# Two layer normalisations scaled on GpSimd instead of VectorE, with re-placed steps, in a fused attention kernel

## The reference, cut to what matters

```
x: (8, 1024, 256) float32
x = x + 0.5 * ffn(layernorm(x))        # "plain" pass, 8 batches
x = x + linear_attn(layernorm(x))      # products without a softmax
x = x + 0.5 * ffn(layernorm(x))        # "plain" pass again, 8 batches

layernorm(x) = (x - mean) / sqrt(var + 1e-5)          # no gain, no bias
ffn(x): q, k, v = x @ Wq, x @ Wk, x @ Wv              # 16 heads of 16
        a = softmax over q of (q k^T / 16)            # 1024 x 1024 per head
        z = a v; z = l2norm(z @ Wo); z = l2norm(z @ Wff); gelu(z)
linear_attn(x): q, k, v of w_qkv; out = (q k^T) v; out @ w_o^T + b_o
```

## Time and profile before

| what | value |
|---|---|
| time, 3 runs | median 2916.42 us (2914.94 to 2917.38) |
| the profiled execution | 2915.55 us, its span 2913.5 us |
| mean granted TensorE clock | 0.987 |
| busy share of the span | PE 92%, DVE 94%, ACT 93%, POOL 26% |

### The profile page before, as it was taken

How to read it: one execution, slowest core, us unless ns; L and a number is a source line. 1 busy time by engine, 2 the same in 40 slices (tenths; PEclk the granted TensorE clock), 3 DMA queues, 4 the chain that set the end, 5 groups by cost and what they waited for, 6 DMA issues and landing times.

```text
span 2913.5 us, 87438 instructions
## 1 busy us (share of the span) xinstructions
PE 2675.2 (92%) x35680; PEld 1077.5 (37%) x35680; DVE 2740.9 (94%) x5574; ACT 2720.2 (93%) x5031; POOL 750.6 (26%) x1181
## 2 busy tenths in 40 slices
...
GB/s 123 52 65 40 55 100 52 68 45 59 103 41 59 65 59 99 37 56 76 59 85 43 54 85 74 89 49 74 61 58 85 74 88 46 64 71 57 74 88 16
DMA packets 151362, 192.89 MB, mean 66 GB/s; under 512 B 34001, under 2 KB 85713, under 8 KB 150962
## 3 DMA queue, kind: packets, MB, share of 16 engines
q1 hardware_dynamic: 150386, 186.13, 31.1%
...
q0 software_dynamic: 576, 1.18, 0.3%
...
## 4 chain that ended last, share of the span: by engine, by line
PE 39%; DVE 36%; ACT 15%; issue 7%; SPq 2%; DMA 0%; POOL 0%; DVEq 0%; ACTq 0%; POOLq 0%
DVE exp_ring L664 30%; PE ring L774 14%; PE ring L828 12%; ACT exp_ring L579 11%; PE o_acc L839 11%; SPq L428 2%; PE ring L879 2%; ACT w_xn L590 1%; DVE bn_stats L704 1%; DVE x_prep L714 1%; DVE bn_stats L718 1%; DVE x_post L686 1%; ACT L590 1%; DVE w_xn L681 1%; DVE exp_rsums L674 1%
## 5 line engine op out<-in xcount | busy, mean ns | idle before, releaser
L664 DVE TENSOR_SCALAR_CACHE_REDUCE exp_ring<-ring 128x1024 f32<-128x1024 f32 x2048 | 2411.9, 1214 | 81.8 <-PE ring L828 74.5
L579 ACT ACTIVATE exp_ring<-exp_ring,neg_max 128x1024 f32<-128x1024 f32 x2048 | 2334.0, 1143 | 109.9 <-DVE exp_ring L664 104.7
L828 PE MATMUL ring<-kq_stack 128*32 128x512 bf16 x16384 | 1186.8, 383 | 172.0 <-DVE exp_ring L664 143.4
L839 PE MATMUL o_acc<-exp_ring,v_scaled 128*32 128x512 f32 x8192 | 1079.0, 599 | 4.8 <-DVE o_T L671 1.9
L828 PEld LDWEIGHTS ring<-kq_stack 128*32 128x32 bf16 x16384 | 409.5, 96 | 1109.0 <-DVE exp_ring L664 538.9
L532 POOL TENSOR_TENSOR v_scaled<-v_now,exp_rsums 128x64 f32<-128x64 f32 x512 | 151.6, 296 | 1911.1 <-DVE exp_rsums L674 1897.8
L579 ACT ACTIVATION_READ_ACCUMULATOR exp_ring<-exp_ring,neg_max 128x1 f32 x2048 | 387.5, 189 | 0.0
L839 PEld LDWEIGHTS o_acc<-exp_ring,v_scaled 128*32 128x32 f32 x8192 | 254.8, 110 | 219.3 <-issue 16.5
L774 PE MATMUL ring<-ffn_wo_wowff,o_T 128*32 128x256 f32 x4096 | 244.4, 380 | 22.3 <-DVE exp_ring L664 11.4
L774 PE MATMUL ring<-xn_T,ffn_wqkv 128*32 128x512 f32 x2048 | 245.0, 598 | 10.8 <-DVE exp_ring L664 9.7
L774 PEld LDWEIGHTS ring<-ffn_wo_wowff,o_T 128*32 128x32 f32 x4096 | 134.2, 110 | 128.2 <-DVE exp_ring L664 29.6
...
## 6 DMA issues: line engine op xcount, KB each, us to landing
...
```

Source lines behind the costliest of these rows:

```text
L579: nc.scalar.activation(e, e, ACT.Exp, bias=negmax[:, i % NM:i % NM + 1], scale=-1.0, accum_out=sums[:, g % EG, c:c + 1]).then_inc(exp_done, 1)
L664: nc.vector.tensor_scalar(E[:, (g % EG) * HQ + c, :].rearrange("p (b n) -> p b n", b=NB), ps, -1.0, None, ALU.mult, ALU.min, accum_out=neg ...
L828: last = mm(ps[k:k + COLS, n, :], kq[:, 0, c, j * P + k:j * P + k + COLS], kq[:, 1, c, n * BANK:(n + 1) * BANK], start=True, stop=True)
L839: last = mm(O[32 * c:32 * c + 32, n, :], vsc[a][:, g % EG, c, :], E[:, (g % EG) * HQ + c, n * BANK:(n + 1) * BANK], start=(a == 0 and j == ...
```

## The change

The `xn` step of phases 1 to 15 (120 instructions) and all `xn2` steps (64) are issued by GpSimd and no longer by VectorE. The eight `xn` of phase 0 stay on VectorE. Since a phase is prepared during the one before, the 120 run in phases 0 to 14, eight in each: 8 in phase 0, 64 in the linear phases, 48 in the plain phases 9 to 14; phase 15 has none. GpSimd adds a negated mean and multiplies by `rstd`; it makes the negated mean itself by one small instruction behind each `rstd` (24 in all), and the semaphore of `rstd` now counts two a step. Nearly all places of the tables and several leads are other numbers. No other instruction is added or removed.

```diff
+        negm = sb("neg_mean", [P, NT])
+        negm2 = sb("neg_mean2", [P, NT])
...
# GpSimd's walk
                 if kind == "ln_rstd":
                     pool.wait_ge(var_ready, p + 1)
                     nc.gpsimd.tensor_tensor(rstd[:], rstd[:], half_neg[:], ALU.pow).then_inc(rstd_ready, 1)
+                    nc.gpsimd.tensor_tensor(negm[:], zero[:, 0:1].to_broadcast([P, NT]), mv[:, :, 0],
+                                            ALU.subtract).then_inc(rstd_ready, 1)
+                elif kind == "xn" and p >= 1:
+                    pool.wait_ge(rstd_ready, (p + 1) * 2)
+                    nc.gpsimd.tensor_scalar(xp[:, i, :], xp[:, i, :], negm[:, i:i + 1], rstd[:, i:i + 1],
+                                            ALU.add, ALU.mult).then_inc(xn_ready, 1)
...
+                elif kind == "xn2":
+                    pool.wait_ge(rstd2_ready, (p + 1) * 2)
+                    nc.gpsimd.tensor_scalar(wb[:, i, 0:D], xr[:, i, :], negm2[:, i:i + 1], rstd2[:, i:i + 1],
+                                            ALU.add, ALU.mult).then_inc(xn2_ready, 1)
...
# VectorE's walk
-                elif kind == "xn":
-                    dve.wait_ge(rstd_ready, p + 1)
+                elif kind == "xn" and p == 0:
+                    dve.wait_ge(rstd_ready, 2)
...
-                elif kind == "xn2":
-                    dve.wait_ge(rstd2_ready, p + 1)
-                    nc.vector.tensor_scalar(wb[:, i, 0:D], xr[:, i, :], mv2[:, i, 0:1], rstd2[:, i:i + 1],
-                                            ALU.subtract, ALU.mult).then_inc(xn2_ready, 1)
...
# LINEAR, two of its lines
-            "xn2": (45.6, 47, 47.2, 47.2, 48.2, 48.2, 49.7, 49.9),
+            "xn2": (43.1, 43.9, 44, 44.2, 45.6, 45.9, 49.6, 50.1),
...
# PLAIN, one of its lines
-            "xn": (33.2, 34.8, 36.6, 45.9, 48.2, 50.9, 51.8, 58.9),
+            "xn": (35.1, 35.9, 42.1, 45.5, 46.3, 46.8, 47, 47),
```

More of the change, by code:

```diff
@@ L67, in build_macaron @@
             "av_next": 2,
[L68 to L76, removed]
-            "xn": (33.2, 34.8, 36.6, 45.9, 48.2, 50.9, 51.8, 58.9),
-            "xt": (60.2, 65.1),
-            "qk": (77.2, 84.4, 93.2, 102.5, 18.2, 24.1, 33.9, 36.1),
@@ L80, in build_macaron @@
[L80 to L87, removed]
+            "z": 4.7,
+            "u": (8.7, 10.9, 12.4, 21.6, 29.9, 42.2, 55.8, 58.2),
+            "u_norm": (63.4,),
+            "w_norm": (66,),
+            "gelu": (67,),
+            "x1": (69.8, 70.4, 72, 72.3),
+            "ln_stats": (5.8, 7.9, 9, 9, 10.5, 10.5, 16.1, 16.2),
@@ new lines, in build_macaron @@
+            "ln_aggr": (25.6,),
+            "ln_rstd": (32.3,),
+            "xn": (35.1, 35.9, 42.1, 45.5, 46.3, 46.8, 47, 47),
+            "xt": (62.2, 66.6),
+            "qk": (76.9, 84.2, 90.1, 101.7, 17.9, 25.6, 33.3, 37.3),
+            "v": (117.8, 123.9, 127.4, 3.4),
+            "load_xp": (3.6,),
+            "stack1": (5.9,),
+            "load_xr": (7.8,),
+            "stack2": (40,),
+            "stack3": (81.5,),
+            "stack0": (107.7,),
+            "store": (113.4,),
@@ L113, in build_macaron @@
[L113 to L124, removed]
+            "w_norm": (32.1,),
+            "gelu": (32.3,),
@@ new lines, in build_macaron @@
+            "ln_stats": (3.9, 12.5, 13.1, 15.6, 16.1, 17.8, 22.2, 23.6),
+            "ln_aggr": (26.6,),
+            "ln_rstd": (29.8,),
+            "xn": (30.7, 32.2, 32.5, 33, 33.8, 33.9, 34.3, 34.6),
+            "xt": (45.4, 47.1),
+            "qk": (79.3, 81.9, 94.9, 98.2, 32.1, 35.9, 38.4, 41.8),
+            "v": (112.9, 124.8, 127.1, 4.3),
+            "load_xp": (0.1,),
+            "stack1": (58.4,),
+            "load_xr": (58.2,),
+            "stack2": (60.2,),
+            "stack3": (79.6,),
@@ L125, in build_macaron @@
+            "stack0": (91.6,),
+            "store": (103.4,),
         },
         "TAIL": {
[L127 to L133, removed]
+            "u": (7.9, 8.9, 14.5, 30.4, 31.7, 51.3, 53.3, 67.3),
+            "u_norm": (17.5, 71.5),
+            "w_norm": (37.3, 76.8),
```

70 lines of the change are left out of this document (36 added, 34 removed).

## The result

The changed kernel takes 2880.16 us, median of 4 runs (2878.12 to 2883.21), the kernel before 2916.88 in its runs beside it: the ratio is 0.9876, 95% interval 0.9859 to 0.9893. That is 36.7 us less; 26 were forecast. The profiled execution took 2880.11 us with a span of 2878.3.

What follows compares the result with a forecast made beforehand. VectorE was taken as the bound where xn and xn2 lie, with ScalarE next and TensorE bounding linear phases from tile 56; 2915.55 - 26.2 + 0.3 = 2889.7 us, stated as 2890, range 2856 to 2923.

Steps and rivals of the forecast that it cites:

- Linear phases: Eight linear phases: 1.6 us gained in tiles 32 to 39, 0.4 in 40 to 47; 2.0 a phase, 16.0 together.
- nothing: Linear phases before tile 32 and after tile 48: no gain.
- Plain phases: Phases 9 to 14, tiles 32 to 63: ScalarE allows 1.4 us; 1.2 taken a phase, 7.2 together.
- the shifts: Other moved places: single steps move by about a tile; counted as zero, uncertain by 1 us a phase either way.
- Phase 0 and the start: Phase 0 gains 3.0 us from eight instructions leaving VectorE; the negated mean adds 0.3 before the first scores.
- The new instruction: Normalisation on GpSimd: 0.41 us each, between 0.20 and 1.17; two pointer operands might cost more.
- D: Linear phases, tiles 32 to 47: GpSimd becomes the bound above 0.65 us an instruction; 2944 us at 1.17; chance 0.17.
- Contention: Linear phases, tiles 32 to 39: VectorE's x1 slows beside GpSimd from 0.69 to 1.24 us, 2.2 a phase at worst.
- Case C: Linear phases: v_scaled 5 us late costs 2 us a phase, cancelling the 16.0; 2906, up to 2920; chance 0.19.
- the sign that the prediction had named for C: av waiting for v_scaled over 2 us a phase while VectorE waits for TensorE.
- Case B: Whole kernel: VectorE's relief of 75.5 us passes through in full, 2841 us, or 2856 with four fifths; chance 0.12.
- the part said to be TensorE's: Linear phases from tile 56 on: TensorE busy 84.8 of 85.4 us, so work taken off VectorE gives nothing.

Runs made afterwards that it cites:

- e2: The changed kernel with the earlier kernel's tables, gaps and leads, except xn at lead 0 and xn2 at lead -1.5 on GpSimd: 2893.54 us, ratio 0.9923.
- e1: The kernel before with the changed kernel's tables, gaps and leads, every normalisation still on VectorE: 2957.25 us, ratio 1.0141.
- e5: e1 with one row moved, xn2 at places 47 to 50.1 instead of 43.1 to 50.1: 2921.77 us, ratio 1.0019.
- e3: The changed kernel with the 64 xn issued during the linear phases back on VectorE: 2899.24 us, ratio 0.9944.
- e6: The changed kernel with the third late qk step of the linear phases at place 39.6 instead of 38.4: 2878.66 us, ratio 0.9869.
- e7: The changed kernel with GpSimd subtracting the mean in xn and xn2 instead of adding the negated mean: 2952.68 us, ratio 1.0126.
- e10: The changed kernel with ScalarE's lead for the qk steps 0.0 instead of 1.0: 2918.97 us, ratio 1.0012.
- e4: The changed kernel with the linear phases' xn spread over places 31.7 to 43 instead of 30.7 to 34.6: 2937.79 us, ratio 1.0077.
- e8: The changed kernel with each of the 120 xn on GpSimd computed twice in place: 2927.08 us, ratio 1.0038.
- e9: The changed kernel with xn and xn2 in several add, multiply and subtract forms, constants or columns as operands, to price each: 2883.47 us.
- e11: e6 with ScalarE's lead for the qk steps 0.5 instead of 1.0: 2906.09 us, ratio 0.9968.
- e12: e6 with two of the linear phases' xn moved from 32.2 and 32.5 to 33.2, behind v_scaled: 2876.9 us, ratio 0.9867.

## Why the prediction was right, and where its steps were not

*The sum.* 26.2 us of gain were forecast, 36.7 came. The direction held, and so did the cause: the engine alone gives 22.6 (e2). How the gain is spread over the stretches did not hold.

*Linear phases, 16.0 forecast, 16.6 measured.* The total is right by luck, since the working is not. The term was 1.6 us in tiles 32 to 39. There the phases 1, 7 and 8 gained 0.9, 0.9 and 0.6, and phases 2 to 6 lost 0.5 to 1.0. ScalarE's 16.2 us were taken as the end of the stretch, but in the changed kernel 17.0 to 17.1 of its busy time fall into it, parts of ten exponentials where it was eight; that left 0.9, and phases 2 to 6, where the clock fell, took longer than before. What made it up lies mostly where the prediction said "nothing": tiles 8 to 31 (1.0 us a phase less), 40 to 55 (1.2 less, 0.4 of it foreseen) and the last eight (0.3 less), against 0.3 more in the first eight. Of the 1.0, 0.6 is there in e2 with the old places: the stretch of the earlier trace rows holds seven `xn`, and the eighth stood ahead of it. By e2 the engine accounts for 1.3 us a phase, the places for the rest, within the 1 us that was allowed for them.

*Plain phases, 7.2 forecast, 17.4 measured.* This is the term that was mis-sized. It was capped by ScalarE's idle time in the earlier trace rows (1.4 us), over tiles 32 to 63 alone. These tiles gave 2.4 us a phase, in e2 as in the changed kernel: they take 39.5 us instead of 41.9, with ScalarE busy for all 39.5 where it was 40.5 before. So its busy time in a window is no fixed demand. In all the engine gives 1.8 us a phase (e2), and 1.1 come from the places, by the difference of 168.9 and 167.8. These 1.1 are in tiles 8 to 31 (1.2 less), which e1 and e5 show too. The prediction put the shifts at "about a tile", but the last plain `xn` moved from place 58.9 to 47 and `stack2` from 66.7 to 40. Tiles 32 to 39 of phase 10 are busy on ScalarE and TensorE from end to end:

```profile
1890.50:1900.80 10.30, 10.30 (x136) 3.64 (x132) 9.57 (x20) 10.30 (x19) 8.20 (x12) 1.00 0.01 2
```

*Phase 0 and the start.* 3.0 less and 0.3 more; measured 2.2 less and 2.1 more. The start cannot be put down to the change: with the changed START table the first tile came at 49.7 to 50.6 us in e1, e3, e5, e6, e7 and e10 and at 47.8 to 48.5 in e4, e8, e9, e11 and e12, and with the old one at 50.2 in e2. One profile of each kernel cannot tell 2 us here.

*The new instruction.* 0.41 us forecast, 0.56 measured: the two column operands, which the text named as the risk, cost 0.15 (e9). It stayed below the 0.65 from which D decides. e7, at 1.22 us, and e8, with each `xn` paid twice, show D's mechanism: they cost the linear phases alone. Where between 0.56 and 1.22 the gain ends, no run shows.

*Contention.* VectorE's two-input `x1` was put at up to 1.24 us, 2.2 us a phase; it took 0.72 in the mean, 0.905 at most, against 0.684 before, 2.1 us in the whole kernel:

```profile
L700 DVE SCALAR_TENSOR_TENSOR x_post<-w_xn,x_post 128x512 f32<-128x512 f32 x64 | 44.7, 717 | 17.5 <-ACT w_xn L604 17.3
```

The contention is there, but mostly on the other side: the five `xn` on GpSimd took 4.09 us instead of 5 x 0.55, because the two that met an `x1` took 1.51 and 0.99; the first split's L420, beside an `x1` as well, took 1.03 instead of 0.62. Of the 120 `xn` of L513, 106 took 0.55 to 0.57 us, nearly all of them beside VectorE's scores. The price that the prediction feared turned up in e7: there two `x1` in each linear phase ran beside the split's L420 and L422, and took 1.12 and 1.64 us. In each of these pairs the instruction that began later grew: the `xn` of 998.55 behind an `x1` of 998.32, in e7 the `x1` of 1034.42 behind an L422 of 1034.04. The Trainium skill's rule (GPSIMD Engine Reference, "Specifications") is that both engines contend when VectorE's instruction has two SBUF inputs; the traces agree. The Trainium skill's advice to keep elementwise work on VectorE ("Engine selection") would have been right for the subtracting form, by e7, and was wrong for the adding one.

*Case C, given 0.19.* Its place and mechanism are in the trace of phase 5: `v_scaled` came 5 us behind its reciprocal, as forecast, `av` waited 2.7 us for it in a linear phase, and VectorE then waited 1.84 us for TensorE. That is the sign that the prediction had named for C, and the gain came all the same: the sign was drawn too wide. C's price did not come. By e12 TensorE is idle there in any case while ScalarE computes the gelu. What differs between the phases is the clock, in the `qk` step that others wait for: over tiles 32 to 47 phase 7 takes 28.5 us at the full clock and phases 3 to 5 29.2 to 29.4. By e6 moving that step removes little of it. Why the clock stayed up in phases 1 and 7 with the same first wait, and fell in 2 to 6, no run settles.

*Case B and the part said to be TensorE's.* Tiles 64 to 127, the window of the earlier trace rows, take 85.2 us, 85.4 before, and tiles 56 to 63 are TensorE's throughout, 11.9 us both times. B did not happen.

*What the prediction did not see.* The two halves of the change need each other. With `xn2` on VectorE the new places cost 41 us (e1), 35 of them by the place of `xn2` alone (e5); on GpSimd they gain some 14.
